# The first attention layer of a two-layer transformer, with four heads in the four row groups of TensorE

## The reference

```
h = layernorm(x)
q, k, v = heads(h @ Wq.T), heads(h @ Wk.T), heads(h @ Wv.T)   # 16 heads of 8 features
scores = q @ k.T / sqrt(8), -inf above the diagonal           # 1024 x 1024 for each of 4 x 16 heads
out = softmax(scores) @ v
x = x + merge_heads(out) @ Wo.T
```

## Time and profile before

| what | value |
|---|---|
| runs, median | 2340.73 us |
| profiled execution, its own time | 2344.26 us |
| its span | 2342.6 us |
| PE busy | 2100.5 us (90%), 11754 instructions |
| DVE busy | 1553.7 us (66%) |
| ACT busy | 1379.9 us (59%) |
| POOL busy | 487.9 us (21%) |
| mean granted TensorE clock | 0.941 of full speed |

### The profile page before, as it was taken

One profiled execution on the slowest core, in us unless ns is written; L12 is line 12 of the kernel. 1 busy time (PEld: TensorE's weight loads), 2 busy tenths in 40 slices (PEclk: granted clock), 3 DMA queues, 4 the chain that ended last, 5 costly groups with the idle time before them and its releaser, 6 DMA issues. The chain is left out here.

```text
span 2342.6 us, 45639 instructions
## 1 busy us (share of the span) xinstructions
PE 2100.5 (90%) x11754; PEld 1367.6 (58%) x11756; DVE 1553.7 (66%) x6216; ACT 1379.9 (59%) x2513; POOL 487.9 (21%) x808
## 2 busy tenths in 40 slices
PE   3489999999973999999977999999999997499998
PEld 2355555555543788888733555555555547378886
DVE  4388778877835677777755666666666633567776
ACT  1246666666663899999842555555555565355554
POOL 4101111111113000000000111111111110267666
PEclk9779999999995999999986999999999998599999
DMA  3523333323301221122167555555555521076553
GB/s 94 181 46 58 45 49 60 54 43 53 47 14 71 55 52 39 36 43 47 18 230 191 123 117 117 116 127 128 128 123 118 116 50 58 23 154 125 131 114 68
DMA packets 96653, 202.86 MB, mean 87 GB/s; under 512 B 14496, under 2 KB 32160, under 8 KB 96032
## 3 DMA queue, kind: packets, MB, share of 16 engines
q1 hardware_dynamic: 96544, 201.65, 38.9%
HBM read 169.47 MB, written 31.60 MB: 86 GB/s over the span
## 5 line engine op out<-in xcount | busy, mean ns | idle before, releaser
L570 DVE CUSTOM_DVE_ANT_0 a1ms<-a1S,mask_q 128x128 bf16<-128x128 f32 (+1 forms) x758 | 387.9, 553 | 182.8 <-issue 179.4
L624 ACT ACTIVATE a1p<-a1T 128x512 f32<-128x512 f32 x576 | 331.4, 597 | 293.8 <-PE a1T L724 293.3
L570 DVE CUSTOM_DVE_ANT_0 a0ms<-a0S,mask_q 128x384 bf16<-128x384 f32 (+2 forms) x752 | 385.8, 553 | 102.3 <-issue 96.9
L624 ACT ACTIVATE a0p<-a0T 128x512 f32<-128x512 f32 x576 | 330.7, 596 | 184.9 <-PE a0T L724 180.8
L703 PE MATMUL a1O<-a1p,a1v 128*33 128x512 f32 (+3 forms) x1536 | 304.2, 496 | 0.9 <-POOL a1p L538 0.9
L1177 DVE TENSOR_TENSOR m_hl<-m_h,m_hh 128x512 fp32r<-128x512 f32 x288 | 197.7, 690 | 116.6 <-ACT m_hh L1133 111.7
L724 PE MATMUL a0T<-a0qT,a0kT 128*128 128x512 f32 (+3 forms) x768 | 261.1, 391 | 3.3 <-DMA a0qT<-a0mr 2.9
L724 PE MATMUL a1T<-a1qT,a1kT 97*128 97x512 f32 (+3 forms) x768 | 262.8, 390 | 0.9 <-DMA a1qT<-a1mr 0.9
L663 PE MATMUL a0S<-a0kS,a0qS 128*128 128x384 f32 (+2 forms) x752 | 227.0, 361 | 32.1 <-DMA a0kS<-scr_k 26.3
L724 PEld LDWEIGHTS a1T<-a1qT,a1kT 97*128 97x128 f32 x768 | 131.6, 189 | 200.7 <-ACT a1p L624 144.5
L663 PE MATMUL a1S<-a1kS,a1qS 96*128 96x128 f32 (+1 forms) x758 | 220.5, 353 | 13.4 <-DMA a1kS<-scr_k 13.2
(11 more groups left out here) (234 smaller groups left out, 3642.4 us busy)
## 6 DMA issues: line engine op xcount, KB each, us to landing
m_gb<-scr_g SPq DMA_DIRECT2D x48, 1024.0 KB, 8.6
a1qS<-scr_q SPq DMA_DIRECT2D x96, 256.0 KB, 6.2
a1qT<-scr_q SPq DMA_DIRECT2D x96, 256.0 KB, 4.1
a1kS<-scr_k SPq DMA_DIRECT2D x96, 128.0 KB, 6.8
a1kT<-scr_k SPq DMA_DIRECT2D x96, 128.0 KB, 4.8
scr_q<-p_hi SPq DMA_DIRECT2D x32, 256.0 KB, 2.4
scr_q<-p_lo SPq DMA_DIRECT2D x32, 256.0 KB, 2.7
a0qS<-scr_q SPq DMA_DIRECT2D x48, 128.0 KB
```

The source lines that it names most:

```text
L570: nc.vector.tensor_tensor_reduce(masked_s[spare][:, 0:c1 - c0], buf[:, 0:c1 - c0], k.mask_q[:, SEQ - w + c0:SEQ - w + c1], 1.0, NEVER, ALU ...
L624: nc.scalar.activation(prob[p % PBUF][:, h, :], t_ps[slot % 2][:, :], ACT.Exp, scale=scale)\
```

## The change

The second attention and all layers behind the first attention stay as they are. For the first attention:

- `project_0` stores hi or lo of q and k three times, in the order in which they are read: (hi, hi, lo) and (hi, lo, hi) in a scratch tensor `[batch, head, 24, SEQ]`. That is seven transfers a supertile.
- The operands are `[P, SEQ]` in three buffers, shared by S and T. Head h has rows 32h to 32h+23, the maximum's row is 32h+24. POOL's memsets are three of 128x1024. A step loads eight times 24 rows (96 KB each) and the values.
- `attention_rows` is new. Both score matmuls take 24 or 25 rows at partition 32h. The whole order is one list over 16 steps, all of it written out, all waits constant. S and T have three banks each; a probability tile has five buffers (three before); the value products of a piece follow three pieces later in one go of up to 512 columns. The S units go block by block with the four heads inside, the maxima of all four heads are merged, turned and copied once a step, and 65 units (48 + 16 + one turn) come ahead of the first T. The unmasked first halves use a plain `tensor_reduce`. At the start 32 matmuls with zeros are issued while the first loads run.
- `project_heads` replaces `project_out`: `attn` is stored as `[P, tiles, 128]` and is turned without staging; no loop.

```diff
-        NSTORE = 5
+        NSTORE = 7
...
-                            for part, tile in ((0, hi[par][n]), (1, lo[par][n])):
-                                sp.dma_start(scr[part, bass.ds(u, 1), :, cols].rearrange("b c n -> (b c) n"),
-                                             tile[:, :].bitcast(F32)).then_inc(stored[par], 16)
+                            for part, tile in enumerate((hi, hi, lo) if n == 0 else (hi, lo, hi)):
+                                sp.dma_start(scr[bass.ds(u, 1), :, part * 8:part * 8 + 8, cols].rearrange("b h r n -> (b h) r n"),
+                                             tile[par][n][:, :].bitcast(F32)).then_inc(stored[par], 16)
...
+T_PIECES = [[(0, 0, 0, 512)], [(0, 0, 512, 1024)], [(0, 1, 128, 512), (384, 3, 384, 512)], [(0, 1, 512, 1024)],
+            [(0, 2, 256, 512), (256, 6, 768, 1024)], [(0, 2, 512, 1024)], [(0, 4, 512, 1024)], [(0, 3, 512, 1024)],
+            [(0, 5, 640, 1024), (384, 7, 896, 1024)]]
+S_BLOCKS = [7, 3, 6, 2, 5, 1, 4, 0]
+WARM = 16
...
+class Rows0:
+    HG, VD, VW, R, NG = 4, 8, 9, 24, BATCH * HEADS // 4
+    S_HEADS = (2, 3, 0, 1)
...
+        self.q, self.k = ([sb(f"a0{n}{i}", [P, SEQ], F32R) for i in range(3)] for n in "qk")
+        self.v = [sb(f"a0v{i}", [P, TPB, 4 * self.VW], F32) for i in range(3)]
...
+    def prepare(self, pool, done):
+        for t in self.k:
+            self.nc.gpsimd.memset(t[:, :].bitcast(F32), 1.0).then_inc(done, 1)
...
+    def max_row(self, g):
+        return self.q[g % 3][self.R:P:32, :]
+
+    def load(self, sp, g):
+        b, hg = divmod(g, 4)
+        for tiles, scr in ((self.q, self.scr_q), (self.k, self.scr_k)):
+            for h in range(4):
+                sp.dma_start(tiles[g % 3][32 * h:32 * h + self.R, :].bitcast(F32), scr[b, 4 * hg + h, :, :]).then_inc(self.loaded[g % 3], 16)
+        sp.dma_start(self.v[g % 3][:, :, :], self.scr_v[b, hg, :, :, :]).then_inc(self.v_loaded[g % 3], 16)
...
+    PBUF, LAG, RING = 5, 3, 3
+    NPC = len(T_PIECES)
+    LEAD, M_AFTER = 4 * HG, HG + 1
...
+    def maxima(g):
+        return [("S", g, h, i, half) for i in S_BLOCKS for half in range(2 if i >= TPB // 2 else 1) for h in rows.S_HEADS]
...
+    before = maxima(0) + lead[1][:M_AFTER] + turned(0) + lead[1][M_AFTER:]
+    beside = []
+    for g in range(NG):
+        row = rest[g + 1] + lead[g + 2][:M_AFTER] + turned(g + 1) + lead[g + 2][M_AFTER:]
+        at = [[] for _ in range(NT)]
+        for n, u in enumerate(row):
+            at[n * NT // len(row)].append(u)
+        for half in range(2):
+            late, p = divmod(closes[half][0] + LAG + 2, NPC)
+            if g >= late:
+                at[p * HG + HG // 2].append(("o", g - late, 0, 0, half))
+        beside.append(at)
...
+                def load(g):
+                    if g >= NG:
+                        return
+                    if g >= 3:
+                        sp.wait_ge(t_ready, (g - 2) * NT)
+                        sp.wait_ge(pv_done, (g - 2) * NPC)
+                    rows.load(sp, g)
+
+                load(0)
+                load(1)
+                for g in range(NG):
+                    sp.wait_ge(m_copied, g + 1)
+                    sp.dma_start(rows.max_row(g).bitcast(F32), mrow[g % 2][:, :].bitcast(F32)).then_inc(row_set[g % 2], 16)
+                    load(g + 2)
...
+                    if n >= RING:
+                        last = units[n - RING]
+                        done = {"S": red_done, "m": m_copied, "o": out_done}[last[0]]
+                        pe.wait_ge(done, count[last[0]][last])
...
+                        ins = nc.tensor.matmul(bank[:, 0:c1 - c0], rows.q_of(g, h, R)[:, i * P:(i + 1) * P],
+                                               rows.k_of(g, h, R)[:, c0:c1], start=True, stop=True)
...
+                        for h in range(HG):
+                            ins = nc.tensor.matmul(o_ps[b][h * CT:h * CT + VW, q0 - b * ST:q1 - b * ST], rows.v_of(g, h, j),
+                                                   prob[(g * NPC + p) % PBUF][:, h, off:off + q1 - q0],
+                                                   start=opens[b] == (p, x), stop=closes[b] == (p, x))
+                    ins.then_inc(pv_done, 1)
...
+                def scores(g, p, h):
+                    n = t_units(g, p) + h
+                    if (p, h) == (0, 0):
+                        pe.wait_ge(row_set[g % 2], 16 * (g // 2 + 1))
+                    if n >= RING:
+                        pe.wait_ge(exp_done, n - RING + 1)
+                    for off, j, q0, q1 in T_PIECES[p]:
+                        ins = nc.tensor.matmul(t_ps[n % RING][:, off:off + q1 - q0], rows.k_of(g, h, R + 1)[:, j * P:(j + 1) * P],
+                                               rows.q_of(g, h, R + 1)[:, q0:q1], start=True, stop=True)
+                    ins.then_inc(t_ready, 1)
+
+                zero = k.mask_q[:, 0:ST]
+                for b in range(2):
+                    for _ in range(WARM):
+                        nc.tensor.matmul(o_ps[b][:, :], zero[:, 0:P], zero, start=True, stop=True)
+                for u in before:
+                    unit(u)
+                for g in range(NG):
+                    for p in range(NPC):
+                        for h in range(HG):
+                            scores(g, p, h)
+                            for u in beside[g][p * HG + h]:
+                                unit(u)
+                        if p >= LAG:
+                            values(g, p - LAG)
+                        else:
+                            values(g - 1, NPC + p - LAG)
...
+                    if c1 < w:
+                        nc.vector.tensor_reduce(mhalf[g % 2][:, h, i - TPB // 2:i - TPB // 2 + 1], bank[:, :], AXX, ALU.max)\
+                            .then_inc(red_done, 1)
+                    else:
+                        nc.vector.memset(held[:, n % 4:n % 4 + 1], 0.0)
+                        nc.vector.tensor_tensor_reduce(dump[n % 4][:, 0:c1 - c0], bank[:, 0:c1 - c0],
+                                                       k.mask_q[:, SEQ - w + c0:SEQ - w + c1], 1.0, NEVER,
+                                                       ALU.add, ALU.max, mmax[g % 2][:, h, i:i + 1]).then_inc(red_done, 1)
+                    if u == maxima(g)[-1]:
+                        dve.wait_ge(red_done, count["S"][u])
+                        upper = mmax[g % 2][:, :, TPB // 2:TPB]
+                        nc.vector.tensor_tensor(upper, upper, mhalf[g % 2][:, :, :], ALU.max).then_inc(merged, 1)
...
+def project_heads(k, name, attn, w, w_loaded=None):
...
+                        for t in range(TPS):
+                            last = nc.tensor.transpose(aT_ps[(s * NC + n) % RING][:, t * P:(t + 1) * P],
+                                                       attn[:, s * TPS + t, n * P:(n + 1) * P], k.ident[:, :])
+                        last.then_inc(turned, 1)
...
-    q0, k0 = (scr(n, [2, BATCH, P, SEQ]) for n in ("scr_q0", "scr_k0"))
+    q0, k0 = (scr(n, [BATCH, HEADS, 24, SEQ]) for n in ("scr_q0", "scr_k0"))
...
-            attn = sb(c, "attn0", [P, 16, TPB, 32])
+            attn = sb(c, "attn0", [P, TILES, D])
+
+            def heads_of(g, half):
+                tile = g // 4 * TPB + half * (TPB // 2)
+                return attn[:, tile:tile + TPB // 2, g % 4 * 32:g % 4 * 32 + 32].rearrange("p i (h c) -> p i h c", h=4)
+
             with ExitStack() as c1:
-                rows = Operands(nc, c1, "a0", 4, 8, False)
+                rows = Rows0(nc, c1, q0, k0, v0)
                 project_0(k, a["L0_attn_q_heads"], a["L0_attn_k_heads"], a["L0_attn_v_heads"], q0, k0, v0, rows)
-                attention(k, "a0", 4, 8, 8.0 ** -0.5, rows, split_rows(q0, 4, 8, (0, 0, 1)), split_rows(k0, 4, 8, (0, 1, 0)),
-                          load_v0, attn)
-            project_out(k, "o0", attn, w_o, 4, w_o_loaded)
+                attention_rows(k, "a0", rows, 8.0 ** -0.5, heads_of)
+            project_heads(k, "o0", attn, w_o, w_o_loaded)
```

More of the change, by code:

```diff
@@ L742, in _, with __init__, q_of, k_of @@
                     unit(units_from([("o", 0, 0, 0)]), before(END)[2:], main_ring(unit_slot(END) + 2), n, END)
+T_PIECES = [[(0, 0, 0, 512)], [(0, 0, 512, 1024)], [(0, 1, 128, 512), (384, 3, 384, 512)], [(0, 1, 512, 1024)],
[6 more added lines that the diff above has]
+    S_HEADS = (2, 3, 0, 1)
+    def __init__(self, nc, c, scr_q, scr_k, scr_v):
+        sb = lambda n, s, d: c.enter_context(nc.sbuf_tensor(n, s, d))
+        self.nc = nc
+        self.q, self.k = ([sb(f"a0{n}{i}", [P, SEQ], F32R) for i in range(3)] for n in "qk")
+        self.v = [sb(f"a0v{i}", [P, TPB, 4 * self.VW], F32) for i in range(3)]
+        self.scr_q, self.scr_k, self.scr_v = scr_q, scr_k, scr_v
+    def prepare(self, pool, done):
+        for t in self.k:
+            self.nc.gpsimd.memset(t[:, :].bitcast(F32), 1.0).then_inc(done, 1)
+    def q_of(self, g, h, n):
+        return self.q[g % 3][32 * h:32 * h + n, :]
+    def k_of(self, g, h, n):
```

(12 more changed lines are left out.)

203 lines of the change are left out of this document (added).

## The result

Four runs of the changed kernel gave 2513.7 to 2515.1 us, median 2514.7; four of the kernel before on the same chip 2336.4 to 2357.6, median 2345.3. The ratio is 1.072 with an interval of 1.068 to 1.076: slower by 7%, where 2226 us and faster were forecast. The profiled execution took 2515.1 us, its span is 2513.4.

A forecast was written before the change was run, and what follows sets the result against it. PE was taken to bound the attention steps, DVE next. Projection -14, before the first S -4.5, maxima +3.4, steps -97 and output projection -2 sum to -114 us: 2230 profiled, so 2226 us forecast, range 2188 to 2282.

The forecast's parts named there:

- rival C: Steps: the clock falls to half, a step takes 54 us, 2640 us in all; chance 0.08, shared with like failures.
- DVE binds, 28.2 us a step: Attention steps: DVE's 24.9 us plus 3 for waits and 0.3 for loads, against 33.6 before; all steps -97 us.
- the starving: Steps: value blocks of 0.92 us hold PE while DVE has at most three full banks; 3 us a step.
- rival A: Steps: the row groups don't overlap, PE's step is 29.8 us, 30.5 with waits, 2258 us in all; chance 0.15.
- B: Steps: operand loads are the bound, PE stands 4.4 us in each of 14 steps, 2288 us in all; chance 0.13.
- D: Steps: DVE binds without gaps, 24.5 us a step, 2174 us in all; chance 0.10.
- Projection: Projection ahead of the attention: 16 us saved with smaller memsets, 2 us lost to more stores; net -14 us.
- memsets' contention: Projection: POOL's memsets slow DVE's normalisations (5.48 us for four, afterwards 1.11); smaller memsets save 16 us in all.
- DMA term: Projection: 16 more stores fill the DMA engines, a supertile needs 5.1 us instead of 4.8; 2 us over eight.
- Before the first S: Start of the attention, now 13.3 us: fewer, faster operand loads, 8.8 us for the zero matmuls; -4.5 us.
- Maxima ahead: Ahead of the first T, DVE-bound: 16 more units of 512 columns, 34.5 us instead of 31.1; +3.4 us.
- Output projection: After the attention steps: two staging copies go at the start; -2 us.

The follow-up runs named there:

- b_rows: The kernel before, with both score matmuls of the first attention over 24 and 25 rows at partition 0 instead of 128: 2724.8 us, ratio 1.152.
- st_full: The changed kernel with all 128 rows in S and T, q in four zero-filled planes, k shared: 2316.3 us, ratio 0.979.
- best_rvf: best_rf with the value products in two parts of 256 columns, two slots apart: 2323.8 us, ratio 0.990.
- st_bf: st_full with probabilities and values in bf16, a probe with coarser output: 2238.8 us, ratio 0.957.
- st_act: st_full with the repeated stores of q and k in the projection issued by ACT instead of SP: 2317.1 us, ratio 0.9865.
- st_w1: st_full with 2 zero matmuls at the start of the attention instead of 32: 2317.3 us, ratio 0.987.
- best_rf: r64_ring plus 128-row zero matmuls ahead of each S before the first T and beside every second T from late step 14 on: 2318.8 us, ratio 0.987.
- fill: The changed kernel with a 128-row, 512-column bf16 matmul of zeros ahead of each S, into the same bank: 3155.3 us, ratio 1.334.
- b64: The kernel before with both score matmuls over 64 rows at partition 0, order and waits untouched: 2465.6 and 2524.8 us.
- r64: st_full with two row groups of 64 rows, two heads each, q in two planes: 2323.2 us, ratio 0.988.
- r64_bf: r64 with probabilities and values in bf16, a probe with coarser output: 2382.3 us, ratio 1.017.
- t_full: The changed kernel with 128 rows in T only, S still 24 rows in four row groups: 2612.0 and 2669.8 us.
- r64_ring: r64 with four banks for S and two for T instead of three and three: 2317.0 us, ratio 0.988.

## Why the prediction was wrong, point by point

- **The clock: the step that failed, and all of the loss.** The steps were costed at 2.4 GHz, with rival C at 0.08 and "against it" the fact that T and value matmuls had brought the clock to 0.99 and kept it there. Those had 128 rows. b_rows, with nothing changed but the rows, shows 0.51; st_full, with nothing changed but the rows back, 1.00. C named two things that might count for little, matmuls of 24 rows and a PE that waits for DVE; the first is shown, the second wasn't needed (in b_rows PE is busy without a gap). Its sign was right. Its 2640 us was for groups that don't overlap; they do, and the time is 2515. C's bound ("slower once a step exceeds 35 us") held: 45. What spoke for C stood in the earlier trace rows: 0.50 in a window in which PE was busy 24 of 31 us. There the matmuls had 128 rows, so it warned of sparse issue and not of narrow rows; I read it as a warm-up.
- **"DVE binds, 28.2 us a step": wrong in size, at either clock.** DVE's work was right, 25.1 us against the forecast 24.9, and the plain reduction costs what the custom one does. What was mis-sized is the starving: 3 us were given for nine blocks. In st_full DVE is idle 7.5 us a step (23% of 32.75). I had counted DVE's stock as three full banks; in the rows of st_full above, the block finds one reduction under way and one full bank. I suppose that T and S waiting for each other in order on PE keep the ring so low; no run shows it alone. Part of the 7.5 is PE's own load, as rival A had it (29.8 + waits): st_full overlaps nothing and took 32.75. With two groups and either a deeper ring or half blocks it was 30.8, with both 29.6 (best_rvf), so about 3 us of the 7.5 are accounted for at full precision; how the rest divides is open, since st_bf, which gives back 5.5, takes work off PE as well.
- **Row groups overlap (A refuted)**: six pieces in 1.22 us at the low clock. A's step without overlap at the high clock, 30.5 us, has its measure in st_full: 32.75. The Trainium skill, TensorE: Matmul & The Clock Gate, "Why this matters for your kernels", recommends it for short contractions and gives 3.07 times the throughput for four; here six pieces took 1.22 us against 6 x 0.43, 2.1 times, at half the clock, so the gain was no more than the loss, and the value products lost without gaining.
- **Loads (B refuted)**: no S waits for a load. At 45 us a step that says little; but st_bf has the same loads of q and k and a step of 27.26 us, under the forecast 28.2, and none of its S waits for one either. **D** never arose.
- **Projection: -3.7 for -14.** The memsets' contention was right (4.80 us from the start, normalisations 1.11 for four). The DMA term was mis-sized: 2 us, then 5.1 a supertile. Measured are about 6. I had scaled 272 GB/s at a share of 75% to 363; the change itself moves 305 at 0.97 and st_act 302 at 0.96. 1.87 MB / 302 GB/s is 6.2 us.
- **Before the first S: -4.8 for -4.5**, 8.5 us from the block's start (93.85 to 102.37), as forecast. The zero matmuls were worth nothing (st_w1, beside st_full).
- **Maxima ahead: +2.2 for +3.4. Output projection and all behind it: -1.3 for -2.** Right within a microsecond or so.

What stays open: by what rule the clock weighs rows against time, and why zeros over 128 rows raise it in one place and not in another (best_rf, best_rvf, fill). b_rows, b64, r64 and r64_bf all have fewer rows at work than before, but no run isolates what is counted. Whether T and S, both in four groups of 24 rows, could hold 2.4 GHz through the steps is not shown by any run; in t_full S did for a while, beside T of 128 rows. The best at full precision is st_full, 2316 us, level with st_w1, st_act and r64_ring: 1.3% faster than the kernel before by st_w1's ratio (0.983 to 0.991), a small gain, and 8 to 9% faster than the change.

## What to carry to other kernels

Before narrowing a matmul to save work, ask what it does to the clock: padding the contraction with zero rows to 128 was worth some 200 us here, more than the overlap of the row groups. A warning can stand in the old trace as a low granted clock beside a busy engine. And where one engine feeds another through a ring, look at the feeder's longest uninterrupted block against what the ring holds when it starts, and at the feeder's total work, together: here removing either alone won at most 0.3 us a step, and both 2 to 3.

## What the runs showed of the hardware that I had not expected

- PE 100% busy with matmuls of 24 and 25 rows has a granted clock of 0.51 (b_rows); with 64 rows there are both levels in one execution (b64, a single trace).
- Two row groups of 64 keep 0.99 beside long fp32 value products and have 0.50 beside short bf16 ones (r64, r64_bf).
- Zero matmuls over 128 rows lift the clock between 64-row matmuls in best_rf (1.00), not in the last step of best_rvf (0.50), and not between 24-row ones (fill, 0.50).
- Alternating 24 and 128 rows costs 0.43 us per 512 columns instead of 0.27 (t_full, st_full, both at the high clock).
- Four bf16 products in four column groups take 0.32 us per 512 columns, four fp32 ones 0.98; the groups run side by side in both, in fp32 in two rounds of four matmuls (st_bf, st_full).
